# Condition matrices loaded in two partition halves, a refilled first projection and nine zero products

## The reference

```
W = cond_weights[condition]                     # 16 matrices of 64x64, one chosen per batch entry
y = einsum('bct,bcd->bdt', x, W)                # x: 64 x 64 x 1024
result = y @ base_w.T + base_b                  # 1024 x 1024
logits = y @ gate_w.T                           # 8 experts, the top 2 kept, softmax over the two
low    = y @ lora_A.T                           # rank 16 for each expert
result += 2 * (low weighted by the gates) @ lora_B
return x + result
```

## Time and profile before

| | |
|---|---|
| median of 3 runs | 478.65 us (478.19 to 480.56) |
| profiled execution | 478.46 us |
| its span of instructions | 476.7 us |
| PE busy | 470.1 us, 99% of the span |
| DVE, ACT, POOL busy | 351.3, 159.6, 119.0 us |
| DMA bytes | 76.9 MB, mean 161 GB/s |

### The profile page before, as it was taken

How to read it: one execution, slowest core, us unless ns; L and a number is a source line. 1 busy time by engine, 2 the same in 40 slices (tenths; PEclk the granted TensorE clock), 3 DMA queues, 4 the chain that set the end, 5 groups by cost and what they waited for, 6 DMA issues and landing times.

```text
span 476.7 us, 8144 instructions
## 1 busy us (share of the span) xinstructions
PE 470.1 (99%) x2660; PEld 460.9 (97%) x2660; DVE 351.3 (74%) x636; ACT 159.6 (33%) x262; POOL 119.0 (25%) x113
## 2 busy tenths in 40 slices
PE   8999999899999999999999999999999999999997
PEld 8999999899999999999999999999999999999996
DVE  4867979887686967869587686867868587585843
ACT  4733444223332422333223332322333223432300
POOL 2345241041320414124041320414114041310400
PEclk9999999999999999999999999999999999999999
DMA  8966533725355262743626346262643626344202
GB/s 312 413 226 223 194 94 132 228 90 192 111 180 188 98 232 56 246 128 132 218 83 206 110 172 202 88 216 70 220 154 133 209 87 212 111 169 120 89 22 88
DMA packets 49275, 76.91 MB, mean 161 GB/s; under 512 B 13666, under 2 KB 32226, under 8 KB 49250
## 3 DMA queue, kind: packets, MB, share of 16 engines
q1 hardware_dynamic: 37586, 71.88, 43.4%
q10 hardware_dynamic: 11664, 4.72, 3.8%
HBM read 41.98 MB, written 34.60 MB: 161 GB/s over the span
## 4 chain that ended last, share of the span: by engine, by line
PE 93%; DVE 4%; DMA 1%; issue 1%; ACT 1%; ACTq 0%; SPq 0%; DVEq 0%
PE acc L902 48%; PE acc L894 27%; PE acc L940 9%; PE mixed L934 8%; DMA x_sb<-in_x_first 1%; DVE x_parts L632 1%; DVE s_lo L676 0%; DVE y_lo L652 0%; DVE y_turned L646 0%; DVE x_sb L761 0%; PE acc L920 0%; DVE t_lo L627 0%; ACT y_hi L520 0%; ACT s_hi L527 0%; PE mixed L920 0%
## 5 line engine op out<-in xcount | busy, mean ns | idle before, releaser
L386 POOL TENSOR_TENSOR x_sb<-x_sb,bias 128x1024 f32<-128x1024 f32 x32 | 77.0, 2429 | 219.8 <-DVE x_sb L744 196.6
L894 PE MATMUL acc<-r_hi,y_lo 128*128 128x392 f32 x256 | 87.0, 340 | 0.2 <-DVE y_lo L611 0.2
L894 PE MATMUL acc<-r_hi,y_hi 128*128 128x392 f32 x256 | 86.9, 339 | 0.0
L894 PE MATMUL acc<-r_lo,y_hi 128*128 128x392 f32 x256 | 86.6, 339 | 0.0
L902 PE MATMUL acc<-t_hi,s_hi 128*128 128x384 f32 x224 | 74.9, 334 | 1.5 <-DVE x_sb L744 1.5
L902 PE MATMUL acc<-t_lo,s_hi 128*128 128x384 f32 x224 | 74.9, 334 | 0.0
L902 PE MATMUL acc<-t_hi,s_lo 128*128 128x384 f32 x224 | 74.8, 334 | 0.0
L902 PE MATMUL acc<-t_lo,y_hi 128*128 128x384 f32 x216 | 72.3, 335 | 0.0
L902 PE MATMUL acc<-t_hi,y_lo 128*128 128x384 f32 x216 | 72.3, 335 | 0.0
L902 PE MATMUL acc<-t_hi,y_hi 128*128 128x384 f32 x216 | 72.2, 334 | 0.0
L375 POOL CAST w_sel<-cw_parts 64x128 fp32r x60 | 39.4, 656 | 103.4 <-PE mixed L934 61.8
(11 more groups left out here) (81 smaller groups left out, 743.6 us busy)
## 6 DMA issues: line engine op xcount, KB each, us to landing
x_sb<-in_x SPq DMA_DIRECT2D x32, 512.0 KB, 4.8
out<-x_sb SPq DMA_DIRECT2D x31, 512.0 KB, 3.1
y_scratch<-y_whole SPq DMA_DIRECT2D x60, 256.0 KB, 2.1
y_moved<-y_scratch SPq DMA_DIRECT2D x120, 128.0 KB, 2.8
t_raw<-in_w_quads SPq DMA_DIRECT2D x4, 768.0 KB, 9.6
scratch<-low_turns ACTq DMA_DIRECT2D x16, 128.0 KB, 1.7
low_turns<-scratch ACTq DMA_DIRECT2D x64, 32.0 KB, 2.5
r_raw<-in_w_plain SPq DMA_DIRECT2D x8, 196.0 KB, 5.5
```

The source lines that it names most:

```text
L386: nc.gpsimd.tensor_tensor(x_sb[:, slot(c), :], x_sb[:, slot(c), :], bias[:, :], ALU.add) \
L894: return nc.tensor.matmul(acc[:, i, 0:NP], y_part[:, i, k, :], w_part[:, k, :], start=(k == 0 and product == 0), stop=(k == KT - 1 and pro ...
```

## The change

The load of cw is cut in two. ACT loads partitions 0 to 63 at the start; SP loads partitions 64 to 127 behind the second x pair, with a semaphore of its own, for which ACT waits before it casts cw. DVE now reads the upper block from partitions 0 to 63. In the first projection PE does three products (0,0), (0 by r_lo) and (1,0) ahead of the wait for y_lo where one stood, and the rest of k = 0 and 1 behind it; the number of products is the same. WARM goes from 12 to 9.

```diff
+        cw_rest_in = sem("cw_rest_in")
...
-        WARM = 12
+        WARM = 9
...
                 if k == 3:
                     sp.dma_start(first_x[:, 1, :], x_first_pairs[1]).then_inc(first_in[1], 16)
+                    sp.dma_start(cw[CH:P, :], cond_w[CH:P]).then_inc(cw_rest_in, 16)
...
-            act.dma_start(cw[:, :], cond_w).then_inc(cw_in, 16)
+            act.dma_start(cw[0:CH, :], cond_w[0:CH]).then_inc(cw_in, 16)
...
                 act.wait_ge(cw_in, 16)
+                act.wait_ge(cw_rest_in, 16)
                 nc.scalar.copy(cw_parts[:, 0, cols], cw[:, cols]).then_inc(cw_hi_ready, 1)
...
-                nc.vector.tensor_copy(w_pair[CH:P, c, CH:P], cw[CH:P, bass.ds(upper[c] * CH, CH)]) \
+                nc.vector.tensor_copy(w_pair[CH:P, c, CH:P], cw[0:CH, bass.ds(upper[c] * CH, CH)]) \
...
-                for k in range(KT):
+                pe.wait_ge(y_hi_ready, 1)
+                pe.wait_ge(r_hi_ready, 1)
+                plain(0, 0, 0, last=1)
+                pe.wait_ge(r_ready, 1)
+                plain(0, 0, 1, last=1)
+                pe.wait_ge(r_hi_ready, 2)
+                plain(0, 1, 0, last=1)
+                pe.wait_ge(y_ready, 1)
+                plain(0, 0, 2, last=1)
+                plain(0, 1, 2, last=1)
+
+                for k in range(2, KT):
                     pe.wait_ge(r_hi_ready, k + 1)
-                    if k % HALF_K == 0:
-                        pe.wait_ge(y_hi_ready, k // HALF_K + 1)
+                    if k == HALF_K:
+                        pe.wait_ge(y_hi_ready, 2)
                     plain(0, k, 0, last=1)
-                    if k % HALF_K == 0:
-                        pe.wait_ge(y_ready, k // HALF_K + 1)
+                    if k == HALF_K:
+                        pe.wait_ge(y_ready, 2)
                     plain(0, k, 2, last=1)
...
-                    if k > 0:
-                        pe.wait_ge(r_ready, k)
-                        plain(0, k - 1, 1, last=1)
+                    pe.wait_ge(r_ready, k)
+                    plain(0, k - 1, 1, last=1)
```

## The result

The changed kernel takes 480.0 us in the median of 7 runs (479.84 to 481.0), the kernel before 478.36 in the median of its 7 runs beside it. The ratio is 1.0035, 95% interval 1.0024 to 1.0045: a loss of 1.6 us, clear of noise and inside 0.5%. The forecast was 479.4 in a range of 478.0 to 480.6. Its direction and the places where time is lost were right; its size, +0.70 us, was less than half of what was measured.

The account below looks back on a forecast made before the run. PE's unbroken stream bounds the kernel, with two tight gates set by the full DMA stream. The head start is lost at gate 1; gate 2 passes on +0.70 us, 478.65 to 479.35, say 479.4 us, range 478.0 to 480.6.

Parts of the forecast that it names:

- gate 1: PE's start on the second pair, needing its y_lo: 0.25 us of slack before, a 0.98 us wait forecast.
- head start: PE's lead before the second pair: 0.24 us from the fill plus 0.29 from earlier x, all lost in the wait.
- Gate 2: PE's weight load for the first expert product, waiting for lowT_lo at 38.44: no slack, PE leaves 0.70 us late.
- step 2 wait: PE's 1.5 us wait for DVE in step 2: claimed to shift with PE and give nothing back.
- D: Delay of loads queued after the second x, +0.70 us; also a rival: clock low much longer, 482.0 us, chance 0.04.
- 262,144 bytes in 0.99 us: Price of either half load of cw, at 266 GB/s taken from two stretches of y_moved loads.
- rival B: Half load of cw: half the partitions give half the rate, delay +1.28 us, time 479.9 us, chance 0.18.
- The page of the Trainium skill named above: "SBUF — State Buffer", Door 1: partitions 0 to 63 load at about half rate; sum +1.28 us instead of +0.70.
- what stands ahead is safe: Start of the stream: x lands 0.29 us earlier, and the second x, less 0.29, is there for its mixing.
- the fill: First projection: three products instead of one before y_lo arrives, second mixing at 9.75 instead of 9.99, gain 0.24 us.
- Rival C: Pause after nine zero products: the clock rises late, near 10.2, costing 1.27 us in all, time 479.9 us, chance 0.07.
- Rival A: Half load of cw at full rate: no delay, gain swallowed or 0.25 us, time 478.4 to 478.65 us, chance 0.29.

Follow-up runs that it names:

- every run of the table: Kernel before plus one 256 KB load behind the second x pair: partitions 64 to 127, 480.10 us; all 128, 479.13; partitions 32 to 95, 479.14.

## Why the prediction was right, and where it was wrong

**Right: what bounds, and gate 1.** The head start ends at y_lo of the second pair (0.81 us of wait, 0.98 forecast). In every run of the table the delay of the fifth r block (1.6, 0.5, 0.7 us), less the 0.2 us by which the gate was open before, came through to PE (16.20, 15.10 and 15.28 against 14.78), and into the medians. Gate 2 asked for more in the changed kernel's profile, as forecast, but not in those of the split alone, of twelve zeros and of the three added loads: there the two weight loads are 0.17 or 0.18 us apart and gate 1 sets the time by itself. The step 2 wait gave nothing back in the changed kernel. It is not fixed, though: over the other profiles it is 1.2 to 2.0 us.

**Wrong: the size of D.** The failed term is "262,144 bytes in 0.99 us" for either part. Both parts cost more: the first 256 KB landed at 0.8 + 4.3 = 5.1, no earlier than the whole had (0.8 + 4.1 = 4.9), and the mixing could start at 6.11, 0.15 earlier than before and not 0.29. A load of the second part's shape put the fifth r block back by 1.6 us where it was added by itself, not by 0.99. D was +1.5 at the fifth r block and +1.7 at lb_raw, not +0.70. That is rival B, given 0.18, and somewhat more than its 1.28. The measured 480.0 lies in the range because B's price was in it, with 0.7 us for a run spread; the forecast's own term does not lead there. The size is less certain than one profile makes it look. Against the kernel before, the fifth r block is late by 1.5 us in the changed kernel, 1.2 in the split alone and 0.8 in the kernel with twelve zeros, and those two profiled executions are among the fastest of their kernels, whose medians are 1.8 and 1.7 us over the kernel before. I took the rate from y_moved loads of 32 partitions, 255 to 277 GB/s, although four of them follow each other and two go to either half of the partitions. That such neighbours overlap and so hide the halving is likely, but no run tests it. The row did not measure the thing it stood in for. The page of the Trainium skill named above, by which the sum was +1.28, came nearer.

**Wrong: what stands ahead is safe.** I moved the second x 0.29 earlier with all that is ahead of the rest of cw. It came 0.6 later, and the second mixing started at 10.24 instead of 9.99, so the head start was gone before gate 1. That the load issued behind it took part of its rate is an inference, and the size varies: the second x is 0.3 later in the profiles of the split alone and of partitions 64 to 127, and not late with twelve zeros in the changed kernel.

**Right but without effect: the fill.** Two products more do stand ahead of the y_lo wait. By itself the fill brought -0.17 us in the median, within its noise; the 0.24 of the forecast is neither shown nor excluded.

**Rival C was undervalued.** It had 0.07. In the changed kernel's profile it did not occur: the mixing records took 2.05 us, and six of its seven runs lie within 0.41 us (the seventh, 481.0, has no profile). Of the three profiles with whole cw and nine zeros it was in two. Of the 24 timed runs with whole cw and nine zeros (with the fill and without), 11 lie at 478.9 or above; of the 66 runs of the kernel before that remain without the 22 named at the start, 10 do. So nine zeros make such runs more frequent; that the clock is behind each of them is seen in two profiles only. The forecast's price of 1.27 us was made for the changed kernel, and no run shows it there. With whole cw it was 1.0, 479.46 against 478.46 for the two profiled executions: the experts started 1.4 late (39.88 against 38.47), and the step 2 wait, 1.2 us for 1.5, gave 0.3 back. What differs between these profiles is whether the pace doubled before PE stopped. In the changed kernel it did, near 4.5 us (its eighteen zero records take 3.90 us, in the two others 4.21), and the pause behind, the longest of the three (1.15 us against 0.62 and 0.79), did no harm. Rival A did not occur, nor did D.

**Open:** why the half loads put the fifth r block back by 0.8 us in one profile and by 1.5 or 1.6 in others, where half the rate makes it 1.28; what makes the clock rise early or late; and what part of the once-loaded cw's saving is lost to the slower start of its stream.

## What to carry to other kernels

Here one load of 256 KB into 64 partitions of one half put the stream back by 1.6 us, more than 512 KB at 410 GB/s take (1.28); splitting by partitions delayed everything behind it and saved next to nothing ahead of it. The same bytes as half the columns of all partitions, or in 64 partitions that cross the middle, put it back by 0.5 and 0.7 us. When the first tens of microseconds are one full stream of transfers, price a change by what it does to the last landing on which the matrix engine waits, since any head start ahead of that is swallowed. Warm-up work should reach the first real work and not go beyond it: three products fewer were worth nothing and risked 1 us, and twelve at the slow pace ran 0.6 us past the landing of x.

## What the runs showed that was not expected

DVE's subtraction of two operands in SBUF stretches to between 2.5 and 4.7 times its length while POOL adds two such operands (1.39 to 3.50 us and 0.54 to 2.56 us). The clock's rise is not fixed to the work: in the profiles with eleven or twelve zeros the mixing took 2.05 to 2.40 us, and with nine it ran at the pace of 1.2 GHz throughout, 3.78 us, in two of them. And a transfer landed up to 0.6 us later when a half load was issued behind it on the same queue.
